# Quantized feed-forward of a decoder: h stored by group, x clipped on GpSimd, neighbouring products interleaved

## The chip, the cores and the metric

One core of one Trainium2 chip runs the whole program in one launch. The metric is the device time of that core in microseconds, the median of several runs. Engines are named as the profile names them: PE (TensorE), DVE (VectorE), ACT (ScalarE), POOL (GpSimd) and SP (SyncE).

## The reference

The model is a chain of six layers on x of 64 x 128 x 128 (batch, tokens, width), each `x = layernorm(x + layer(x))`. The change touches the last layer alone, a feed-forward in which activations and weights are rounded to 8-bit steps. The scale of an activation is one number for the whole tensor, so its maximum must be known before any of it is rounded:

```
def _act_fake_quant(x, clip_factor):
    scale = sigmoid(clip_factor) * max(abs(x)) / 127
    return clip(round(x / scale), -128, 127) * scale
def _weight_fake_quant(w):                      # one scale a row
    scale = max(abs(w), axis=1, keepdims=True) / 127
    return clip(round(w / scale), -128, 127) * scale
xq   = _act_fake_quant(x, clip_x)
gate = xq @ wq(w_gate).T ; up = xq @ wq(w_up).T       # 128 -> 352
h    = _act_fake_quant(silu(gate) * up, clip_down)    # needs the maximum over all h
y    = h @ wq(w_down).T                               # 352 -> 128
x    = layernorm(x + y)
```

## The kernel before, in words

The layers run one after the other; `quantized` is the last. All of its x (64 batches) stays in SBUF with tokens on the partitions: `xs` is [128 tokens, 64, 128]. The work is cut into NG = 16 groups of GB = 4 batches, GT = 512 columns a group. The inner width 352 is cut into IC = 3 chunks of up to 128 rows.

After the weights are rounded and the scale of x is known (`scale_of`, `s_k`), the **first half** runs over the groups. For each group:

- DVE clips x in two passes (`quantize_x`): L2489 multiplies by the inverse scale (a pointer scalar) and takes the minimum with 127 into `xt`; L2491 takes the maximum with -128 and adds a large constant that makes the addition round. There is one `xt`, so group g waits until ACT has read g-1 (`s_xq`).
- ACT subtracts the constant and writes bf16 (`rounded`, L2420, into `xqb`); PE turns it (`turned`, L2360); ACT copies it out of the bank (`copied`, L2414, into `xT`, two buffers).
- PE makes gate and up products of chunk c in banks 2 + 2c and 3 + 2c (`gate_up`, L2367 and L2368). It waits until the up product on DVE of the same chunk of the group before has freed the banks (`s_h`).
- ACT takes tanh of half the gate (L2426, into `th`, one buffer a chunk, also freed by `s_h`).
- DVE multiplies (tanh + 1) by the gate product from its bank into `t1` (L2541, the gate product below), then `t1` by a scale and the up product from its bank into h (L2543, the up product below). `t1` is one buffer: the up product waits for the gate product just ahead of it, and the next gate product for that up product.
- DVE takes the largest magnitude of the group's h (L2545).

On ACT the order in a group is tanh 0 to 2, copy of x of g+1, rounding of x of g+2. On DVE it is both passes over x of g+2, then gate and up product of chunk 0, of chunk 1, of chunk 2, then the maximum. POOL has nothing to do in this half. Each engine runs two groups unrolled, then a hardware loop over pairs of groups, then the last two unrolled; inside the loop the counts waited for and the addresses by group are worked out in registers.

h is kept for all groups: `h` is [128, 3 chunks, 8192 tokens] and `hg` its view by group, so a group's h is three runs of 512 in each partition, 8192 apart.

When the last maximum is there, the scale of h is worked out (`prologue2`), and the **second half** runs over the groups again: DVE clips h in two passes as it did x (`shift`, L2562 and L2564, into `ht`, two buffers, one run of 1536 each), ACT rounds to bf16 (`whole`, L2447), PE makes the down product (`down`, L2391), DVE scales it out of the bank (L2574), POOL adds it to x (`add`, L2609), DVE takes mean and variance (`stats`: L2584, L2589, L2593, L2594), POOL makes the inverse root with a pow (L2614) and the shift with a multiply (L2617), ACT applies them (`normed`, L2454, four groups later), and SP stores the group. DVE's order in a group g is `shift` of g+1, the scaling of g, `stats` of g-1; POOL's is `add` of g, then pow and multiply of g-1.

Of the kernel before, what the change touches and what calls it, by code (L numbers as in the profile page):

```python
# [9 lines left out]
ALU = mybir.AluOpType  # L10
ACT = mybir.ActivationFunctionType
AX = mybir.AxisListType
# [2222 lines left out]
def quantized(nc, const, banks, x, y, a):  # L2235
# [13 lines left out]
    with ExitStack() as st:  # L2249
        def sb(name, shape, dt=F32):  # L2250
            return st.enter_context(nc.sbuf_tensor(f"q_{name}", shape, dt))

        def sem(name, per=1):
            return Count(nc.alloc_semaphore(f"q_{name}"), per)
# [25 lines left out]
        xqb = sb("xqb", [P, GT], BF16)  # L2280
        xT = sb("xT", [P, 2, GT], BF16)
        th = sb("th", [P, IC, GT])
        t1 = sb("t1", [P, GT])
        h = sb("h", [P, IC, B * S])
        ht = sb("ht", [P, 2, IC, GT])
        hq = sb("hq", [P, 2, IC, GT], BF16)
        r = sb("r", [P, 2, GT])
# [5 lines left out]
        s_w = sem("weights"); s_setup = sem("setup"); s_sig = sem("sigmoid_exp"); s_wq = sem("weights_quantized")  # L2293
        s_wt = sem("weights_turned", 2); s_wT = sem("weights_copied", 2); s_top = sem("top", 3); s_tt = sem("top_turned", 3)
        s_t1 = sem("top_reduced", 3); s_tb = sem("top_spread", 3); s_k = sem("scales_ready")
        s_xs = sem("x_shifted"); s_xq = sem("x_quantized"); s_hm = sem("h_max"); s_xt = sem("x_turned"); s_xT = sem("x_copied")
        s_gu = sem("gate_up", IC); s_th = sem("tanh", IC); s_h = sem("h", IC)
        s_hs = sem("h_shifted"); s_hq = sem("h_quantized"); s_y = sem("down"); s_yr = sem("down_read"); s_add = sem("x_added")
        s_bn = sem("out_stats"); s_ag = sem("out_mean"); s_ov = sem("out_var"); s_pw = sem("out_pow"); s_op = sem("out_scales")
# [8 lines left out]
        o_g = y.rearrange("(g b) t d -> g t b d", b=GB)  # L2308
        xg = xs[:].rearrange("p (g b) d -> p g (b d)", b=GB)
        xs_g = xs[:].rearrange("p (g b) d -> p g b d", b=GB)  # L2310
        hg = h[:].rearrange("p c (g t) -> p g c t", t=GT)
        block = st.enter_context(nc.Block())

        @block.sync
# [152 lines left out]
        def _(dve):  # L2467
# [16 lines left out]
                v.reciprocal(inv[:, n:n + 1], scl[:, n:n + 1]).then_inc(ch.sem, 1)  # L2484
                v.wait_ge(ch.sem, ch.next())

            def quantize_x(v, ch, g):
                v.wait_ge(s_xq.sem, s_xq.at(g))
                v.tensor_scalar(xt[:], xg[:, g, :], inv[:, 0:1], QMAX, ALU.mult, ALU.min).then_inc(ch.sem, 1)  # L2489
                v.wait_ge(ch.sem, ch.next())  # L2490
                v.tensor_scalar(xt[:], xt[:], -QMAX - 1.0, MAGIC, ALU.max, ALU.add).then_inc(s_xs.sem, 1)  # L2491

            def prologue(v, ch):
                v.wait_ge(s_w.sem, 16 * NW)
                v.wait_ge(s_setup.sem, s_setup.at(1))
                v.tensor_reduce(wamax[:, 0:2 * IC], wgu[:], AX.X, ALU.max, apply_absolute_value=True)
                v.tensor_reduce(wamax[:, 2 * IC:], wd[:], AX.X, ALU.max, apply_absolute_value=True).then_inc(ch.sem, 1)
                v.wait_ge(ch.sem, ch.next())
                v.tensor_scalar(wscale[:], wamax[:], 1.0 / QMAX, None, ALU.mult).then_inc(ch.sem, 1)
                v.wait_ge(ch.sem, ch.next())  # L2500
                v.reciprocal(winv[:], wscale[:]).then_inc(ch.sem, 1)
                v.wait_ge(ch.sem, ch.next())
                for c in range(2 * IC):
                    whole(v, ch, wq[:, c, :], wgu[:, c, :], wgu[:, c, :], winv[:, c:c + 1]).then_inc(ch.sem, 1)
                    v.wait_ge(ch.sem, ch.next())
                whole(v, ch, wdq[:], wd[:], wd[:], winv[:, 2 * IC:]).then_inc(ch.sem, 1)
                v.wait_ge(ch.sem, ch.next())
                for n in range(2):
                    ins = v.memset(wq[IL:P, n * IC + 2, :], 0.0)
                ins.then_inc(s_wq.sem, 1)  # L2510
                v.wait_ge(s_sig.sem, s_sig.at(1))
                v.tensor_scalar(sig[:], sig[:], 1.0, None, ALU.add).then_inc(ch.sem, 1)
                v.wait_ge(ch.sem, ch.next())
                v.reciprocal(sig[:], sig[:]).then_inc(ch.sem, 1)
                v.wait_ge(ch.sem, ch.next())
                for c in range(LC):
                    v.wait_ge(s_ld[c].sem, s_ld[c].at(16))
                    ins = v.tensor_reduce(xmax[:, c:c + 1], xs[:, c * B // LC:(c + 1) * B // LC, :].rearrange("p b d -> p (b d)"),  # L2518
                                          AX.X, ALU.max, apply_absolute_value=True)
                ins.then_inc(ch.sem, 1)  # L2520
                v.wait_ge(ch.sem, ch.next())
                scale_of(v, ch, 0, xmax[:])
                v.tensor_scalar(kt[:], wscale[:, 0:IC], scl[:, 0:1], 0.5, ALU.mult, ALU.mult).then_inc(ch.sem, 1)
                v.wait_ge(ch.sem, ch.next())
                v.tensor_scalar(kk[:], wscale[:, IC:2 * IC], scl[:, 0:1], None, ALU.mult).then_inc(ch.sem, 1)
                v.wait_ge(ch.sem, ch.next())
                v.tensor_tensor(kk[:], kk[:], kt[:], ALU.mult).then_inc(s_k.sem, 1)
                v.wait_ge(s_k.sem, s_k.at(1))
                quantize_x(v, ch, 0)
                quantize_x(v, ch, 1)  # L2530

            def turn(v, ch, i):
                last = isinstance(i, int) and i == TURNS - 1
                for l in range(2):
                    g = 2 * i + l
                    if not last:
                        quantize_x(v, ch, g + 2)
                    for c in range(IC):
                        v.wait_ge(s_th.sem, s_th.at(g, c + 1))
                        v.wait_ge(s_h.sem, s_h.at(g, c))  # L2540
                        v.scalar_tensor_tensor(t1[:], th[:, c, :], 1.0, banks[2 + 2 * c], ALU.add, ALU.mult).then_inc(ch.sem, 1)  # L2541
                        v.wait_ge(ch.sem, ch.next())
                        v.scalar_tensor_tensor(hg[:, g, c, :], t1[:], kk[:, c:c + 1], banks[3 + 2 * c], ALU.mult, ALU.mult).then_inc(s_h.sem, 1)  # L2543
                    v.wait_ge(s_h.sem, s_h.at(g + 1))
                    v.tensor_reduce(hmax[:, bass.ds(g, 1)] if not isinstance(g, int) else hmax[:, g:g + 1],  # L2545
                                    hg[:, g, :, :], AX.XY, ALU.max, apply_absolute_value=True).then_inc(s_hm.sem, 1)
            looped(dve, s_dve, TURNS, 2 * (1 + IC), prologue, turn, lambda v, ch: None)

            def prologue2(v, ch):
                v.wait_ge(s_hm.sem, s_hm.at(NG))  # L2550
# [47 lines left out]
        def _(pool):  # L2598
# [4 lines left out]
            pool.memset(magic[:], -MAGIC).then_inc(s_pool, 1)  # L2603
            pool.wait_ge(s_pool, 3)
            pool.sem_inc(s_setup.sem, 1)
            def add(g, l):
                pool.wait_ge(s_yr.sem, s_yr.at(g + 1))
                pool.sem_inc(s_step, 1)
                pool.tensor_tensor(xg[:, g, :], xg[:, g, :], r[:, l], ALU.add).then_inc(s_add.sem, 1)  # L2609

            def scales(g, l):
                pool.wait_ge(s_ov.sem, s_ov.at(g + 1))
                pool.sem_inc(s_step, 1)
                pool.tensor_tensor(osc[:, g, 0, :], ovar[:, l, 0, :], half_pow[:, 0:GB], ALU.pow).then_inc(s_pw.sem, 1)  # L2614
                pool.wait_ge(s_pw.sem, s_pw.at(g + 1))
                pool.sem_inc(s_step, 1)
                pool.tensor_tensor(osc[:, g, 1, :], osc[:, g, 0, :], ovar[:, l, 1, :], ALU.mult).then_inc(s_op.sem, 1)  # L2617
            add(0, 0)
            add(1, 1)
            scales(0, 0)  # L2620
# [119 lines left out]
```

## Time and profile before

| what | value |
|---|---|
| median of 3 runs (lowest to highest) | 5442.49 us (5440.62 to 5445.76) |
| profiled execution, its time | 5428.83 us |
| profiled execution, span of the core | 5427.1 us |
| busy over the span: DVE / PE / POOL / ACT | 4319.6 (80%) / 4056.8 (75%) / 3163.7 (58%) / 2781.0 (51%) us |
| first half of the last stage, from the scale of x to the last maximum of h | 5208.9 to 5332.5 us |
| second half, to the end of the span | 5332.5 to 5427.0 us |

The profile is of one execution. Most of the span belongs to the five layers ahead; the two last lines are the stretches that the change touches. A busy share over the whole span says little about them, so they are read by stretch and in order of time.

### The profile page before, as it was taken

How to read it: one execution, taken by the hardware profiler on the slowest of the kernel's cores; microseconds unless marked ns; L12 is line 12 of the kernel's file. 1: busy time of each engine (PE TensorE's matmuls, PEld its weight loads, DVE VectorE, ACT ScalarE, POOL GpSimd, SP SyncE). 2: the span in 40 equal slices, each digit the busy share in tenths (PEclk: the TensorE clock that was granted, in tenths of full speed). 3: DMA queues.
4: the chain of work that ended last, by engine and by line, in shares of the span. 5: the costliest groups of instructions: out<-in, count | busy, mean ns of one | idle time of the engine just before them, and what ended most of it. 6: DMA issues, size and time to landing. Idle time of an engine off the chain costs nothing. (4 is left out here: it accounts for less than half of the span.)

```text
span 5427.1 us, 104523 instructions
## 1 busy us (share of the span) xinstructions
PE 4056.8 (75%) x29692; PEld 2331.6 (43%) x29692; DVE 4319.6 (80%) x8453; ACT 2781.0 (51%) x6469; POOL 3163.7 (58%) x3426
## 2 busy tenths in 40 slices
PE   5878778887787778874888678883747788688843
PEld 2333333333333333332666456652735666466611
DVE  5999999999999999994888767763356777666678
ACT  4555555555555555552777534434654445344434
POOL 5888888878888888874777533326452222333302
PEclk8998999889989989986999889995877888799955
DMA  2111111111110111102655366544125555465511
GB/s 84 67 49 54 69 68 68 42 62 69 68 69 33 69 68 68 69 37 46 105 102 102 60 119 110 104 88 151 57 89 107 95 96 95 82 112 102 98 39 31
DMA packets 320209, 420.99 MB, mean 78 GB/s; under 512 B 40000, under 2 KB 301712, under 8 KB 309136
## 3 DMA queue, kind: packets, MB, share of 16 engines
q1 hardware_dynamic: 315536, 408.35, 32.3%
q0 software_dynamic: 4352, 8.95, 0.5%
q8 instruction: 128, 2.10, 0.2%
q14 instruction: 193, 1.58, 0.1%
HBM read 307.65 MB, written 109.58 MB: 77 GB/s over the span
## 5 line engine op out<-in xcount | busy, mean ns | idle before, releaser
L2202 POOL TENSOR_TENSOR m_h<-m_dtu,m_Bb 128x512 f32<-128x512 f32 x1024 | 1598.1, 1590 | 148.4 <-PE bank L1835 146.1
L1835 PE MATMUL bank<-m_h,ident 128*128 128x512 f32 x2048 | 1245.2, 699 | 404.5 <-DVE m_h L2101 398.8
L1835 PEld LDWEIGHTS bank<-m_h,ident 128*128 128x128 f32 x2048 | 370.6, 210 | 1083.8 <-DVE m_h L2101 931.3
L2095 DVE TENSOR_TENSOR_SCAN m_h<-m_dA,m_h 128x512 f32<-128x512 f32 x512 | 771.0, 1506 | 0.5
L2101 DVE TENSOR_TENSOR m_h<-m_h,bank 128x512 f32<-128x512 f32 x1024 | 672.1, 656 | 14.4 <-PE bank L1828 14.4
L2095 DVE TENSOR_TENSOR_SCAN m_h<-bank,m_h 128x512 f32<-128x512 f32 x512 | 620.4, 1212 | 16.5 <-ACT bank L1983 9.5
L1983 ACT ACTIVATE bank<-m_dt,m_A 128x512 f32<-128x512 f32 x512 | 352.5, 688 | 378.6 <-DVE m_h L2095 273.6
L1983 ACT ACTIVATE m_dA<-m_dt,m_A 128x512 f32<-128x512 f32 x512 | 366.9, 717 | 350.1 <-DVE m_h L2095 343.4
L688 DVE TENSOR_REDUCE x_nm<-bank 128x4 f32<-128x308 f32 x512 | 242.7, 474 | 184.0 <-PE bank L359 181.1
L531 ACT ACTIVATE x_sm<-bank,x_nm 128x77 f32<-128x77 f32 x1024 | 318.2, 336 | 62.5 <-DVE x_nm L688 62.1
L688 DVE TENSOR_REDUCE f_nm<-bank 128x4 f32<-128x512 f32 x256 | 175.7, 687 | 120.2 <-PE bank L359 119.1
L521 ACT ACTIVATE a_pT<-bank 128x512 f32<-128x512 f32 x256 | 152.9, 598 | 219.5 <-PE bank L379 217.0
L1779 PE MATMUL bank<-m_xTp,m_wck 128*128 128x512 f32 x512 | 255.0, 602 | 12.6 <-ACT m_xTp L1897 12.6
L521 ACT ACTIVATE f_pT<-bank 128x512 f32<-128x512 f32 x256 | 153.0, 598 | 216.4 <-PE bank L379 215.7
L521 ACT ACTIVATE x_pT<-bank 77x512 f32<-77x512 f32 x256 | 151.9, 593 | 216.5 <-PE bank L379 213.6
L896 POOL TENSOR_TENSOR x_var<-x_var,half_pow 128x1 f32<-128x1 f32 x128 | 70.5, 550 | 304.2 <-DVE x_var L742 304.2
L876 POOL TENSOR_TENSOR x_sm<-x_sm,x_gp 128x308 f32<-128x308 f32 x256 | 203.1, 798 | 71.9 <-ACT x_sm L531 71.4
L401 PE MATMUL bank<-x_pT,x_vB 128*32 128x128 f32 x4096 | 220.3, 288 | 6.9 <-ACT x_ou L540 6.6
L896 POOL TENSOR_TENSOR a_var<-a_var,half_pow 128x1 f32<-128x1 f32 x64 | 35.3, 551 | 324.8 <-DVE a_var L742 324.8
L688 DVE TENSOR_REDUCE a_nm<-bank 128x4 f32<-128x512 f32 x256 | 175.2, 685 | 60.5 <-PE bank L359 45.8
L531 ACT ACTIVATION_READ_ACCUMULATOR x_sm<-bank,x_nm 128x1 f32 x1024 | 221.6, 216 | 0.0
L1828 PE MATMUL bank<-m_Cs,m_selC 80*128 80x512 bf16 x512 | 213.5, 417 | 0.0
(425 smaller groups left out, 10366.2 us busy)
## 6 DMA issues: line engine op xcount, KB each, us to landing
m_Bb<-m_B SPq DMA_DIRECT2D x32, 4096.0 KB, 12.2
x_Ks<-x_k_parts SPq DMA_DIRECT2D x32, 462.0 KB
x_q_parts<-x_qp SPq DMA_DIRECT2D x32, 384.0 KB, 4.0
x_Qs<-x_q_parts SPq DMA_DIRECT2D x32, 384.0 KB
f_Ks<-f_k_parts SPq DMA_DIRECT2D x16, 768.0 KB
a_Ks<-a_k_parts SPq DMA_DIRECT2D x16, 768.0 KB
x_xp<-x_stage SPq DMA_DIRECT2D x32, 256.0 KB
x_Qs<-x_q_parts SPq DMA_DIRECT2D x32, 256.0 KB
```

Source lines behind the costliest of these rows:

```text
L401: ins = pe.matmul(bankO[j * VT:(j + 1) * VT, half * S:(half + 1) * S], vB[:, lb % 2, 4 * c + j, :], pT[:, lb % 2, 4 * c + j, :], start=(c ...
L521: act.activation(pT[0:sk, p, 4 * c:4 * c + 4, :].rearrange("p h t -> p (h t)"), src, ACT.Exp).then_inc(s_e.sem, 1)
L531: ins = act.activation(sm[:, lm % 2, h, :], bankS[c % 2][:, (h - 4 * c) * S2:(h - 4 * c + 1) * S2], ACT.Exp, bias=nm[:, lm % 2, 0, h:h + 1 ...
L688: v.tensor_reduce(nm[:, p, 0, 4 * c:4 * c + 4], src, AX.X, ALU.max, negate=True).then_inc(ready.sem, 1)
L876: pool.tensor_tensor(ws, ws, gp[:, lm // GB, lm % GB, :].unsqueeze(1).to_broadcast([P, 4, S2]), ALU.mult).then_inc(s_pg.sem, 1)
L1779: ins = pe.matmul(o, wck[:, d, part, c * P:(c + 1) * P], xTp[:, :, part:part + S], start=(part == 0), stop=(part == CK - 1))
L1828: pe.matmul(banks[2 + s % 2], selC[:, s, :], Cs[:, d, :], start=True, stop=True).then_inc(s_C.sem, 1)
L1835: pe.matmul(banks[4 + c], ident[:], h[:, k % RING, :], start=(s == 0), stop=(s == NS - 1)).then_inc(s_ya.sem, 1)
L1983: act.activation(decays[k % AHEAD], dt[:, d, c, :], ACT.Exp, scale=A[:, d, c, s:s + 1]).then_inc(s_dA.sem, 1)
L2095: v.tensor_tensor_scan(h[:, k % RING, :], decays[k % AHEAD], h[:, k % RING, :], 0.0, ALU.mult, ALU.add).then_inc(s_h.sem, 1)
L2101: v.tensor_tensor(h[:, k % RING, :], h[:, k % RING, :], banks[2 + s % 2], ALU.mult).then_inc(s_hC.sem, 1)
L2202: pool.tensor_tensor(h[:, k % RING, :], dtu[:, d, c, :], Bb[:, d, s, :], ALU.mult).then_inc(s_dB.sem, 1)
```

## The change: what it does

- `h` is allocated as [128, group, chunk, 512] in place of [128, chunk, 8192]: a group's h is one run of 1536 in each partition. The view `hg` is that tensor now.
- `quantize_x` moves from DVE to POOL, with the same two passes and one more semaphore (`s_xc`) between them. POOL waits for the scales (`s_k`) and then runs all 16 groups, unrolled, before its part of the second half. `xt` remains one buffer.
- `t1` gets one buffer a chunk. DVE's order in a group becomes gate 0, maximum of the group before, gate 1, up 0, gate 2, up 1, up 2. The last maximum follows after the loop.
- The gate product of chunk c now waits for `s_h` of the same chunk of the group before.

```diff
-        t1 = sb("t1", [P, GT])
-        h = sb("h", [P, IC, B * S])
+        t1 = sb("t1", [P, IC, GT])
+        hg = sb("h", [P, NG, IC, GT])
...
-        hg = h[:].rearrange("p c (g t) -> p g c t", t=GT)
...
-            def quantize_x(v, ch, g):            # and its calls on DVE
-                v.wait_ge(s_xq.sem, s_xq.at(g))
-                v.tensor_scalar(xt[:], xg[:, g, :], inv[:, 0:1], QMAX, ALU.mult, ALU.min).then_inc(ch.sem, 1)
-                v.wait_ge(ch.sem, ch.next())
-                v.tensor_scalar(xt[:], xt[:], -QMAX - 1.0, MAGIC, ALU.max, ALU.add).then_inc(s_xs.sem, 1)
...
+            def largest(v, g):
+                v.wait_ge(s_h.sem, s_h.at(g + 1))
+                v.tensor_reduce(hmax[:, bass.ds(g, 1)] if not isinstance(g, int) else hmax[:, g:g + 1],
+                                hg[:, g, :, :], AX.XY, ALU.max, apply_absolute_value=True).then_inc(s_hm.sem, 1)
 
             def turn(v, ch, i):
-                last = isinstance(i, int) and i == TURNS - 1
                 for l in range(2):
                     g = 2 * i + l
-                    if not last:
-                        quantize_x(v, ch, g + 2)
-                    for c in range(IC):
+                    ready = [None] * IC
+
+                    def times_gate(c):
                         v.wait_ge(s_th.sem, s_th.at(g, c + 1))
-                        v.wait_ge(s_h.sem, s_h.at(g, c))
-                        v.scalar_tensor_tensor(t1[:], th[:, c, :], 1.0, banks[2 + 2 * c], ALU.add, ALU.mult).then_inc(ch.sem, 1)
-                        v.wait_ge(ch.sem, ch.next())
-                        v.scalar_tensor_tensor(hg[:, g, c, :], t1[:], kk[:, c:c + 1], banks[3 + 2 * c], ALU.mult, ALU.mult).then_inc(s_h.sem, 1)
-                    v.wait_ge(s_h.sem, s_h.at(g + 1))
-                    v.tensor_reduce(...)
-            looped(dve, s_dve, TURNS, 2 * (1 + IC), prologue, turn, lambda v, ch: None)
+                        v.wait_ge(s_h.sem, s_h.at(g - 1, c + 1))
+                        v.scalar_tensor_tensor(t1[:, c, :], th[:, c, :], 1.0, banks[2 + 2 * c], ALU.add, ALU.mult).then_inc(ch.sem, 1)
+                        ready[c] = ch.next()
+
+                    def times_up(c):
+                        v.wait_ge(ch.sem, ready[c])
+                        v.scalar_tensor_tensor(hg[:, g, c, :], t1[:, c, :], kk[:, c:c + 1], banks[3 + 2 * c], ALU.mult, ALU.mult).then_inc(s_h.sem, 1)
+
+                    times_gate(0)
+                    if not (isinstance(g, int) and g == 0):
+                        largest(v, g - 1)
+                    for c in range(1, IC):
+                        times_gate(c)
+                        times_up(c - 1)
+                    times_up(IC - 1)
+            looped(dve, s_dve, TURNS, 2 * IC, prologue, turn, lambda v, ch: largest(v, NG - 1))
...
+            def quantize_x(g):                   # on POOL
+                pool.wait_ge(s_xq.sem, s_xq.at(g))
+                pool.tensor_scalar(xt[:], xg[:, g, :], inv[:, 0:1], QMAX, ALU.mult, ALU.min).then_inc(s_xc.sem, 1)
+                pool.wait_ge(s_xc.sem, s_xc.at(g + 1))
+                pool.tensor_scalar(xt[:], xt[:], -QMAX - 1.0, MAGIC, ALU.max, ALU.add).then_inc(s_xs.sem, 1)
...
+            pool.wait_ge(s_k.sem, s_k.at(1))
+            pool.sem_inc(s_step, 1)
+            for g in range(NG):
+                quantize_x(g)
             add(0, 0)
             add(1, 1)
```

## Rows read from the trace of the kernel before

**Rows 1.** The two halves: us, each engine's busy us (instructions), clock, DMA share, GB/s

```profile
5208.90:5332.50 123.60, 56.09 (x160) 14.73 (x160) 108.99 (x146) 52.23 (x80) 0.00 (x0) 0.50 0.00 0
...
5332.50:5427.00 94.50, 25.12 (x198) 20.35 (x198) 78.11 (x215) 50.06 (x80) 39.83 (x48) 0.50 0.16 45
```

**Rows 2.** DVE's groups in both halves: count, busy us, mean ns, idle before, releaser

```profile
L2543 DVE SCALAR_TENSOR_TENSOR q_h<-q_t,q_kk,bank 128x512 f32 (+1 forms) x48 | 35.9, 747 | 6.2 <-DVE q_t L2541 5.7
L2541 DVE SCALAR_TENSOR_TENSOR q_t<-q_th,bank 128x512 f32<-128x512 f32 x48 | 32.9, 686 | 4.2 <-ACT q_th L2426 0.7
L2562 DVE TENSOR_SCALAR q_ht<-q_h,q_inv 128x1536 f32 (+1 forms) x16 | 29.0, 1810 | 1.2 <-issue 1.1
L2545 DVE TENSOR_REDUCE q_hmax<-q_h (+1 forms) x16 | 28.1, 1753 | 1.8
L2564 DVE TENSOR_SCALAR q_ht<-q_ht 128x1536 f32<-128x1536 f32 x16 | 15.4, 960 | 0.6
```

**Rows 3.** DVE's timeline, one steady group of the first half: start us, us

```profile
5241.09 1.75 DVE L2545 TENSOR_REDUCE q_hmax<-q_h  x1
...
5243.28 0.43 DVE L2491 TENSOR_SCALAR q_xt<-q_xt 128x512 f32<-128x512 f32 x1
5243.62 0.68 DVE L2541 SCALAR_TENSOR_TENSOR q_t<-q_th,bank 128x512 f32<-128x512 f32 x1
5244.46 0.75 DVE L2543 SCALAR_TENSOR_TENSOR q_h<-q_t,q_kk,bank 128x512 f32 x1 [0.16 <-DVE q_t L2541]
...
5248.75 1.75 DVE L2545 TENSOR_REDUCE q_hmax<-q_h  x1
```

**Rows 4.** Timeline of PE and ACT after an up product of chunk 0

```profile
5245.26 0.61 PE L2367 MATMUL bank<-q_xT,q_wT 128*128 128x512 bf16 x1 [2.78 <-DVE q_h L2543]
5245.66 0.63 PE L2368 MATMUL bank<-q_xT,q_wT 128*128 128x512 bf16 x1
5246.33 0.69 ACT L2426 ACTIVATE q_th<-bank,q_kt 128x512 f32<-128x512 f32 x1 [1.87 <-PE bank L2368]
```

**Rows 5.** Timeline of the first half's start, from the first pass over x

```profile
5208.95 0.49 DVE L2489 TENSOR_SCALAR q_xt<-q_x,q_inv 128x512 f32<-128x512 f32 x1
...
5211.96 0.71 ACT L2420 ACTIVATE q_xqb<-q_xt,q_magic 128x512 bf16<-128x512 f32 x1
...
5213.19 0.69 ACT L2426 ACTIVATE q_th<-bank,q_kt 128x512 f32<-128x512 f32 x1 [0.52 <-PE bank L2368]
...
5213.91 0.69 DVE L2541 SCALAR_TENSOR_TENSOR q_t<-q_th,bank 128x512 f32<-128x512 f32 x1 [0.26 <-ACT q_th L2426]
```

**Rows 6.** POOL's groups over the whole span: an addition, a pow, a memset

```profile
L2609 POOL TENSOR_TENSOR q_x<-q_x,q_r 128x512 f32 x14 | 17.8, 1270 | 26.1 <-DVE q_r L2574 26.1
...
L2614 POOL TENSOR_TENSOR q_osc<-q_ovar,half_pow 128x4 f32 x14 | 14.3, 1020 | 5.4 <-DVE q_ovar L2594 5.4
...
L1442 POOL MEMSET moe_go_on<- 128x512 f32 x1 | 0.5, 525 | 0.1
```

**Rows 7.** Timeline of one steady group of the second half

```profile
5353.44 1.81 DVE L2562 TENSOR_SCALAR q_ht<-q_h,q_inv 128x1536 f32 x1
5353.77 1.02 POOL L2614 TENSOR_TENSOR q_osc<-q_ovar,half_pow 128x4 f32 x1 [0.41 <-DVE q_ovar L2594]
...
5355.29 0.96 DVE L2564 TENSOR_SCALAR q_ht<-q_ht 128x1536 f32<-128x1536 f32 x1
...
5358.71 1.81 DVE L2562 TENSOR_SCALAR q_ht<-q_h,q_inv 128x1536 f32 x1 [0.22 <-issue]
```

**Rows 8.** Timelines of two earlier stages where DVE and POOL run together

```profile
3119.16 1.15 POOL L848 TENSOR_TENSOR f_qp<-f_qr,f_qp 128x512 bf16<-128x512 f32 x1
3119.23 1.36 DVE L654 CAST f_qp<-f_qr 128x512 bf16<-128x512 f32 x1 [1.04 <-POOL f_qr L841]
...
3674.49 1.01 POOL L1450 TENSOR_TENSOR moe_scales<-moe_norm,half_pow 128x4 f32 x1
3674.70 0.17 DVE L1272 TENSOR_SCALAR moe_norm<-moe_stats 128x4 f32<-128x4 f32 x1 [0.26 <-DVE moe_stats L1266]
```

More of the change, by code:

```diff
@@ L2295, in quantized @@
         s_t1 = sem("top_reduced", 3); s_tb = sem("top_spread", 3); s_k = sem("scales_ready")
-        s_xs = sem("x_shifted"); s_xq = sem("x_quantized"); s_hm = sem("h_max"); s_xt = sem("x_turned"); s_xT = sem("x_copied")
+        s_xc = sem("x_clipped"); s_xs = sem("x_shifted"); s_xq = sem("x_quantized"); s_hm = sem("h_max"); s_xt = sem("x_turned"); s_xT = sem("x_copied")
         s_gu = sem("gate_up", IC); s_th = sem("tanh", IC); s_h = sem("h", IC)
@@ L2527, in prologue @@
                 v.tensor_tensor(kk[:], kk[:], kt[:], ALU.mult).then_inc(s_k.sem, 1)
-                v.wait_ge(s_k.sem, s_k.at(1))
-                quantize_x(v, ch, 0)
-                quantize_x(v, ch, 1)
+            def largest(v, g):
+                v.wait_ge(s_h.sem, s_h.at(g + 1))
+                v.tensor_reduce(hmax[:, bass.ds(g, 1)] if not isinstance(g, int) else hmax[:, g:g + 1],
+                                hg[:, g, :, :], AX.XY, ALU.max, apply_absolute_value=True).then_inc(s_hm.sem, 1)
@@ L2532, in turn @@
             def turn(v, ch, i):
-                last = isinstance(i, int) and i == TURNS - 1
                 for l in range(2):
                     g = 2 * i + l
-                    if not last:
-                        quantize_x(v, ch, g + 2)
-                    for c in range(IC):
+                    ready = [None] * IC
+                    def times_gate(c):
                         v.wait_ge(s_th.sem, s_th.at(g, c + 1))
-                        v.wait_ge(s_h.sem, s_h.at(g, c))
-                        v.scalar_tensor_tensor(t1[:], th[:, c, :], 1.0, banks[2 + 2 * c], ALU.add, ALU.mult).then_inc(ch.sem, 1)
-                        v.wait_ge(ch.sem, ch.next())
-                        v.scalar_tensor_tensor(hg[:, g, c, :], t1[:], kk[:, c:c + 1], banks[3 + 2 * c], ALU.mult, ALU.mult).then_inc(s_h.sem, 1)
-                    v.wait_ge(s_h.sem, s_h.at(g + 1))
-                    v.tensor_reduce(hmax[:, bass.ds(g, 1)] if not isinstance(g, int) else hmax[:, g:g + 1],
-                                    hg[:, g, :, :], AX.XY, ALU.max, apply_absolute_value=True).then_inc(s_hm.sem, 1)
```

## The prediction, made before the result was known

> **What bounds the kernel now.** The change touches only the last stage, the quantized feed-forward. Its work after the scale of x falls into two halves, the last 218 us of the span [rows 1]. In the first (123.6 us: gate and up products, all maxima) DVE works 109.0 us, ACT 52.2, PE 56.1 and POOL nothing. In the second (94.5 us: rounding h, the down product, the norm) DVE works 78.1, ACT 50.1, POOL 39.8. The reader should see in both that DVE is the engine with no time to spare and that POOL is free in the first. TensorE's granted clock is 0.50 in both, its 1.2 GHz level. The groups by line [rows 2] say what DVE does there: in the first half, for each of 16 groups, three gate products of 0.686 us, three up products of 0.747, one maximum of 1.753, and two passes over x; in the second, the clip of h at 1.810 and its second pass at 0.960, though both treat 1536 elements a partition.
>
> DVE's order of time for one steady group [rows 3] shows a period of 7.66 us, 5241.09 to 5248.75. Two things make it: 0.48 + 0.43 us for x ([rows 5] has the first pass, [rows 3] the second), and gaps. Where nothing has to be waited for, the next instruction starts about 0.08 before the last one's end (5243.28 + 0.43 = 5243.71, next start 5243.62). Where the up product waits for the gate product just ahead, it starts 0.16 after the end instead (5243.62 + 0.68 to 5244.46). The group has three such pairs.
>
> **The change part by part: first half.**
>
> *x to POOL.* 32 passes leave DVE: 0.43 + 0.345 (0.43 less the 0.08 of overlap, as for the next) + 0.085 of hand-over between them, 0.86 us a group.
>
> *Interleaving and the late maximum.* The up product now follows the next chunk's gate product, and the maximum of group g-1 stands behind the first gate product of g, so no DVE instruction waits for the one just ahead. The group becomes a sum of unwaited starts: 3 x 0.686 + 3 x 0.747 + 1.753 - 7 x 0.08 = 5.49 us. t1 grows to one buffer a chunk, so its reuse no longer waits either.
>
> *What is late next.* Bank pair 0 and th 0 come free when up product 0 ends. From there [rows 4]: PE starts 0.06 later (5245.26 after an end at 5244.46 + 0.75 [rows 3]), its second product ends 1.03 after that, ACT's tanh starts 0.04 later and takes 0.69, and about 0.05 hands it to DVE: 1.87 us. Meanwhile DVE has gate 2, up 1 and up 2 left, 0.606 + 0.667 + 0.667 = 1.94. That is nearly a tie: the ring of up 0, PE, tanh, gate 0, maximum, gate 1, up 0 is also 5.5 us round. Chunks 1 and 2 have over 3 us. The copy and the rounding of x stand ahead of that tanh on ACT: tanh 2 ends 1.85 us after the group's start by [rows 4], the copy is no longer than a tanh, the rounding takes 0.71 [rows 5], so ACT is free at about 3.25, before up 0 ends at 3.63. A tie with register waits in a loop will not be met each time; I take 5.6, with 5.49 below and 5.95 above (the 0.16 stall back at each of three gate products).
>
> *POOL's passes.* No pass with one tensor input at 128x512 f32 by POOL stands in the trace. The nearest rows [rows 6]: a memset of that shape 0.525 us, an addition of two tensors 1.27. I take 0.9, the middle. The Trainium skill, GPSIMD Engine Reference, section Engine selection, holds that POOL is about half as fast as DVE on two inputs but near line rate on one; an estimate from that would be about 0.5 us a pass and 1 us less at the start; no row here shows it. In the loop POOL needs 2 x 0.9, ACT's rounding 0.72 (xt has one buffer) and some 0.2 of hand-over, 2.7 of 5.6 us: hidden. DVE's instructions in this half each read at most one tensor from SBUF besides the bank, and none shows the halved time of a clip pass, so I let them and POOL run beside each other at their own durations. Not hidden is the start. POOL begins where DVE did (5208.95), but ACT has the rounding of group 1 ahead of the first tanh, and it now waits for four POOL passes and two roundings: 5208.95 + 4 x 0.9 + 2 x 0.72 + 0.5 of hand-overs = 5214.5, against 5213.19 [rows 5]. That is 1.3 us late (0.15 at 0.525 a pass, 2.8 at 1.27).
>
> *Sum of the half.* First gate product at 5213.91 + 1.3 = 5215.2; group 1 starts 4.1 later (gate 1 waits for a tanh 0.85 behind the first, the pace of a PE pair; then 0.606 + 0.747 to the end of up 0 and 1.87 for the ring); 14 periods of 5.6 are 78.4; the last group and its maximum, which now has nothing behind it, 5.6 + 1.75 = 7.35: end at 5305.1. Before, the half ended at 5332.5 [rows 1]. Saved: 27.4 us (bounds: 5.49 and 0.15, 30.1; 5.95 and 2.8, 21.0).
>
> **The change: second half.** With h as [group, chunk, token], the clip reads one run of 1536 where it read three runs of 512, 8192 apart, while its destination is one run as before. The second pass, one run in and out, takes 0.960, just over half the clip's 1.810 [rows 2]; and x, one run too, was clipped with the same pointer scalar in 0.48 where the pass with constants took 0.43 [rows 5, 3]. So the clip should take 0.960 + 0.05 = 1.01: 0.80 less. A group lasts 5.27 (5353.44 to 5358.71 [rows 7]; of 16, every other one is some 0.2 shorter), nearly all DVE; without 0.80 it is some 4.35. ACT's work there is 50.1/16 = 3.1 a group and POOL's 39.8/16 = 2.5, so DVE stays the limit. Of 16 clips that of group 1 is lost in a wait for the first down product; 15 x 0.80 = 12.0.
>
> What speaks against it is POOL. The pow of the norm starts 0.33 us after the clip does [rows 7]. At the old rate they ran side by side. At the halved rate DVE and POOL exclude each other in this trace: a CAST of 512 elements, work of some 0.43 (as the second pass over x [rows 3]), took 1.36 behind a POOL tensor_tensor that had started 0.07 before it [rows 8]. But another DVE tensor_scalar, 0.2 us into a pow of the same 128x4 shape, took 0.17 [rows 8]; a pow on four elements mostly computes, so it should give way. I allow 0.07 a group for pow's reads: 11 us saved.
>
> The Trainium skill, SBUF — State Buffer, section Who interferes with whom, is stricter: a DVE instruction in a two-port mode and a POOL instruction exclude each other for the whole instruction, and whoever issues first goes first. By that rule the clip would run, then pow with the second pass waiting for all of it. The CAST row agrees with that, the tensor_scalar inside the pow does not; what it would make of the time is the first rival below.
>
> **Sum.** 27.4 + 11 = 38.4 us. The profiled execution took 5428.83 (span 5427.1 and 1.7 around it), so it would take 5390. The median of the runs, 5442.49, lies 13.7 above that execution; nothing in the rows ties that difference to this stage, so I carry it: 5404.
>
> **Rivals.**
>
> 1. *POOL's pow holds the second half.* Pow waits for the clip (1.01), then the second pass waits for pow's 1.02: the group gains 0.80 and loses about 1.02, 0.2 x 15 = 3 us worse than before in that half. For: the CAST row. Against: the tensor_scalar row. Saved 27.4 - 3 = 24: 5418.
> 2. *The ring takes DVE's place in the first half.* Each hand-over in the loop costs 0.1 to 0.2 more (ACT and PE wait on registers too), period 6.2: 14 x 0.6 = 8.4 less saved, 30.0: 5412. For: the tie above, and the 0.16 gaps. Against: [rows 4] already hold the loop's hand-overs.
> 3. *The slower side: POOL's clip is too slow.* The group is then 2T + 0.72 + 0.2. It passes the old 7.66 at T = 3.4 us a pass, and at 3.7 it eats the second half's gain too. For: pow takes 1.02 us for four elements [rows 6], so POOL can be slow by operation. Against: multiply-, add- or subtract-like tensor_tensors keep 1.27 for 512. At T = 5: 16 x 3.3 = 52 lost, 11 gained: 5483.
> 4. *The clip doesn't change its rate* (the layout was not the reason): 27.4 saved, 5415.
>
> **How the numbers follow.** Forecast 0.62 (own range 5398 to 5410), rival 1 0.16, rival 2 0.11, rival 3 0.03, rival 4 0.05, rivals 1 and 2 together 0.03 (27.4 - 8.4 - 3 = 16 saved, 5426). Both halves at their best, 30.1 + 12.0, give 5400; the three runs spread over 5 us, so the range begins at 5397, and it ends with rivals 1 and 2 together, 5425. A measurement can tell about 0.2%, 11 us, from no change. All cases but rival 3 save more than that; faster 0.95, same 0.02, slower 0.03.
>
> **What would show it.** DVE's idle before the up products (5.7 us before) near zero and none of its passes on x; starts of successive maxima 5.5 to 5.7 apart; first tanh 1 to 2 us later after the scales; POOL's passes 0.5 to 1.3 each; the clip of h at about 1.01 and groups of the second half 4.3 to 4.5 apart, with pow lengthened instead. A second pass of h of about 2 us shows rival 1; DVE idle before the first gate product of each group, released by tanh, shows rival 2; ACT's rounding waiting for POOL throughout, rival 3; a clip of 1.8 with no POOL beside it, rival 4. The prediction is wrong if the first half saves under 21 us or the second loses.

## The result, and the profile after

The changed kernel took 5410.6 us, the median of six runs (5403.87 to 5429.04), against 5444.12 for the kernel before on the same chip (six runs, 5434.42 to 5452.83). The ratio is 0.9943 with a 95% interval of 0.9925 to 0.9961: 0.6% less time, a small gain but clear of no change. The forecast was 5404, its range 5397 to 5425.

Runs of either kernel scatter by some 20 us, most of it from the layers ahead: in ten of the eleven traces the scales of the last stage come anywhere from 5204.8 to 5232.8 us, while the changed kernel's two traces agree within 0.1 us in each half. So the two halves of the last stage are compared inside each trace. One run, the version without interleaving below, took 6430.81 us with its layers ahead at a lower granted clock (0.55 over the whole run, 0.87 in the others), and only its last stage is read. The first fence answers to [rows 1]: each stretch, busy us of PE, PEld, DVE, ACT and POOL with instructions, granted clock, DMA share, GB/s.

```profile
5218.46:5318.40 99.94, 51.36 (x160) 16.05 (x160) 87.75 (x113) 50.52 (x80) 62.89 (x32) 0.57 0.00 0
5318.40:5402.13 83.73, 25.13 (x198) 20.36 (x198) 66.57 (x215) 50.03 (x80) 49.14 (x48) 0.50 0.18 50
```

The first half went from 123.55 to 99.91 us, the second from 94.66 to 83.76 (ends taken to the nanosecond): 23.6 and 10.9, together 34.5. POOL, idle in the first half before, now works 62.9 us of it. The groups of the changed kernel answer to [rows 2] and, for POOL, to [rows 6].

```profile
L2540 DVE SCALAR_TENSOR_TENSOR q_h<-q_t,q_kk,bank 128x512 f32 (+1 forms) x48 | 34.2, 741 | 0.0
L2535 DVE SCALAR_TENSOR_TENSOR q_t<-q_th,bank 128x512 f32<-128x512 f32 x48 | 32.6, 680 | 12.1 <-ACT q_th L2425 11.5
L2610 POOL TENSOR_SCALAR q_xt<-q_x,q_inv 128x512 f32<-128x512 f32 x16 | 32.0, 2002 | 45.1 <-DVE q_kk L2520 26.1 <-ACT q_xqb L2419 18.9
L2612 POOL TENSOR_SCALAR q_xt<-q_xt 128x512 f32<-128x512 f32 x16 | 30.9, 1929 | 1.4
L2564 DVE TENSOR_SCALAR q_ht<-q_h,q_inv 128x1536 f32 (+1 forms) x16 | 16.4, 1027 | 1.3 <-issue 1.1
L2566 DVE TENSOR_SCALAR q_ht<-q_ht 128x1536 f32<-128x1536 f32 x16 | 16.3, 1019 | 0.5
```

The idle time before the up products (L2540) is gone, 6.2 us before; the clip of h (L2564) takes 1.03 for 1.81. But a pass over x takes POOL 2.00 and 1.93 us, and DVE idles 12.1 before gate products. Most of that is one wait, at the start. The timeline there answers to [rows 5]: start us, us, idle before in brackets.

```profile
5218.69 2.00 POOL L2610 TENSOR_SCALAR q_xt<-q_x,q_inv 128x512 f32<-128x512 f32 x1 [26.12 <-DVE q_kk L2520]
...
5225.71 1.93 POOL L2612 TENSOR_SCALAR q_xt<-q_xt 128x512 f32<-128x512 f32 x1
...
5227.67 0.72 ACT L2419 ACTIVATE q_xqb<-q_xt,q_magic 128x512 bf16<-128x512 f32 x1 [2.78 <-POOL q_xt L2612]
5228.30 1.82 ACT L2425 ACTIVATE q_th<-bank,q_kt 128x512 f32<-128x512 f32 x3
...
5229.00 1.28 DVE L2535 SCALAR_TENSOR_TENSOR q_t<-q_th,bank 128x512 f32<-128x512 f32 x2 [10.54 <-ACT q_th L2425]
...
5232.54 0.72 ACT L2419 ACTIVATE q_xqb<-q_xt,q_magic 128x512 bf16<-128x512 f32 x1 [1.93 <-POOL q_xt L2612]
```

The first tanh waits for four POOL passes and two roundings. The first gate product comes 10.54 us after the scales; before it was 5.0. Group 1 is late as well: on ACT the rounding of group 2's x stands ahead of group 1's tanh, and it waits 1.93 us for POOL's third pair of passes.

Two groups further on stand for the steady state; they answer to [rows 3 and 4].

```profile
5259.52 0.61 PE L2366 MATMUL bank<-q_xT,q_wT 128*128 128x512 bf16 x1 [1.88 <-DVE q_h L2540]
...
5259.98 1.40 DVE L2540 SCALAR_TENSOR_TENSOR q_h<-q_t,q_kk,bank 128x512 f32 x2
5260.69 0.69 ACT L2425 ACTIVATE q_th<-bank,q_kt 128x512 f32<-128x512 f32 x1 [1.65 <-PE bank L2367]
...
5261.52 0.69 DVE L2535 SCALAR_TENSOR_TENSOR q_t<-q_th,bank 128x512 f32<-128x512 f32 x1
...
5265.18 0.39 PE L2366 MATMUL bank<-q_xT,q_wT 128*128 128x512 bf16 x1 [2.09 <-DVE q_h L2540]
...
5265.64 1.40 DVE L2540 SCALAR_TENSOR_TENSOR q_h<-q_t,q_kk,bank 128x512 f32 x2
5265.82 0.69 ACT L2425 ACTIVATE q_th<-bank,q_kt 128x512 f32<-128x512 f32 x1 [1.26 <-PE bank L2367]
...
5266.95 0.68 DVE L2535 SCALAR_TENSOR_TENSOR q_t<-q_th,bank 128x512 f32<-128x512 f32 x1
```

Follow chunk 0 twice. At the 1.2 GHz level a product takes 0.61; the tanh that needs the pair ends at 5260.69 + 0.69 = 5261.38, when DVE's last up product is just over (5259.98 + 1.40), and gate 0 starts 0.14 later. In the next group the product takes 0.39, the tanh ends at 5266.51, and gate 0 starts 0.09 before its predecessor's end. But the clock is only one of two things that decide. Here are the stretches from maximum to maximum, these two groups and the one ahead of them:

```profile
5251.02:5256.47 5.45, 3.37 (x11) 1.04 (x10) 5.45 (x9) 3.23 (x6) 3.85 (x3) 0.50 0.00 0
5256.47:5262.12 5.65, 3.55 (x12) 1.13 (x11) 5.51 (x8) 3.27 (x6) 4.23 (x3) 0.50 0.00 0
5262.12:5267.55 5.43, 2.69 (x12) 0.84 (x11) 5.43 (x8) 3.36 (x6) 3.83 (x3) 0.81 0.00 0
```

The first stretch is at 0.50 too, and yet it is 5.45 long. There the tanh of chunk 0 follows PE's second product more closely:

```profile
5254.47 0.63 PE L2367 MATMUL bank<-q_xT,q_wT 128*128 128x512 bf16 x1
...
5255.14 0.69 ACT L2425 ACTIVATE q_th<-bank,q_kt 128x512 f32<-128x512 f32 x1 [1.46 <-PE bank L2367]
```

It starts 0.04 after that product's end and ends at 5255.83, 0.10 before DVE's last up product, so gate 0 has nothing to wait for. In the group of 5.65 it starts 0.13 after the product. This goes by the place in the hardware loop, each turn of which does two groups: all through the loop's twelve groups the tanh of a turn's first group starts 0.13 after PE, that of its second 0.04. So the tie that the prediction named is there. It is lost in the first group of a turn at 0.50 (5.65 or 5.66 us, four of the six). It is won where PE made chunk 0's products at the 2.4 GHz level (the other two), and in the second group of every turn at either clock (5.43 to 5.45). Before, the whole half was at 0.50 [rows 1].

The second half shows one odd group and two steady ones; they answer to [rows 7].

```profile
5328.52 1.01 DVE L2564 TENSOR_SCALAR q_ht<-q_h,q_inv 128x1536 f32<-128x1536 f32 x1
5328.78 1.86 POOL L2617 TENSOR_TENSOR q_x<-q_x,q_r 128x512 f32<-128x512 f32 x1 [26.86 <-DVE q_r L2576]
5329.56 1.90 DVE L2566 TENSOR_SCALAR q_ht<-q_ht 128x1536 f32<-128x1536 f32 x1
...
5337.99 1.02 DVE L2564 TENSOR_SCALAR q_ht<-q_h,q_inv 128x1536 f32 x1
5338.31 1.73 POOL L2622 TENSOR_TENSOR q_osc<-q_ovar,half_pow 128x4 f32 x1 [0.41 <-DVE q_ovar L2596]
5339.05 0.96 DVE L2566 TENSOR_SCALAR q_ht<-q_ht 128x1536 f32<-128x1536 f32 x1
...
5342.46 1.05 DVE L2564 TENSOR_SCALAR q_ht<-q_h,q_inv 128x1536 f32 x1 [0.23 <-issue]
5342.50 1.05 POOL L2622 TENSOR_TENSOR q_osc<-q_ovar,half_pow 128x4 f32 x1 [0.36 <-DVE q_ovar L2596]
5343.55 0.96 DVE L2566 TENSOR_SCALAR q_ht<-q_ht 128x1536 f32<-128x1536 f32 x1
5343.81 0.75 POOL L2625 TENSOR_TENSOR q_osc<-q_osc,q_ovar 128x4 f32 x1 [0.26 <-POOL q_osc L2622]
```

Steady groups come in two kinds, in turn. In the first, POOL's pow starts 0.32 into the clip and takes 1.73. It ends 1.03 us after the clip does, as long as a whole pow of before (1.02), but also 0.03 after the second pass, which ran at its own 0.96 beside it; these rows don't tell for which of the two it waited. In the second kind pow starts 0.04 after the clip does, and both take 1.05, so neither waited more than 0.03 for the other. There the multiply behind pow is the one that is longer, 0.75 for 0.20, and it ends 0.05 after the second pass. In both kinds POOL waits, and DVE's passes keep their time within 0.03. Groups last 4.28 and 4.47 in turn, 5.04 and 5.26 before. The odd group is the third: there POOL's first addition, 512 elements, starts inside the clip, and the second pass takes 1.90. That happens once and costs 0.9 us.

### The profile page after: what moved, and what is told of

Its sections match the earlier page's. It is cut to its first block and busy times, and to the rows that moved or that the text cites. A ratio compares the mean times of both kernels' runs of the same rounds, so it can differ in the third digit from the quotient of the medians.

```text
span 5402.1 us, 104475 instructions
## 1 busy us (share of the span) xinstructions
PE 4058.6 (75%) x29692; PEld 2332.1 (43%) x29692; DVE 4293.4 (79%) x8421; ACT 2777.7 (51%) x6469; POOL 3230.1 (60%) x3458
## 6 DMA issues: line engine op xcount, KB each, us to landing
m_Bb<-m_B SPq DMA_DIRECT2D x32, 4096.0 KB, 12.1
```

## The experiments

Each is a version of the changed kernel. Where only one execution was taken, its total says little (the scatter above), so the verdicts go by the stretches in its trace, from the scales to the last maximum and from there to the end, in us. Steady groups are those of the hardware loop; "5.43 or 5.66" stands for 5.43 to 5.46 and 5.64 to 5.67.

| run | first half | second half | steady group, first half |
|---|---|---|---|
| before | 123.55 | 94.66 | 7.66 |
| changed | 99.91 | 83.76 | 5.43 or 5.66 |
| first three groups of x on DVE | 93.42 | 83.72 | 5.43 or 5.66 |
| all of x on DVE | 103.47 | 83.70 | 6.29 |
| gate and up of a chunk together | 105.24 | 83.77 | 5.91 |
| old layout of h | 99.82 | 94.59 | 5.43 or 5.66 |
| maximum in its own group | 100.68 | 83.71 | 5.65 |
| other operations in POOL's passes | 99.05 | 83.77 | 5.43 or 5.66 |
| an addition ahead of pow | 99.90 | 103.08 | 5.43 or 5.66 |
| first three on DVE, up 0 earlier | 92.18 | 83.72 | 5.43 |
| changed, again | 99.85 | 83.77 | 5.43 or 5.66 |

**The start.** DVE does both passes for groups 0 to 2 ahead of its loop, POOL the rest.

```diff
+    FIRST = 3
...
+                for g in range(FIRST):
+                    quantize_v(v, ch, g)         # DVE, after kk
...
-            for g in range(NG):
+            for g in range(FIRST, NG):
                 quantize_x(g)                    # POOL
```

> The changed kernel with x of groups 0, 1 and 2 clipped by DVE at the start as in the kernel before, POOL from group 3 on. Theory: POOL's passes of 2.0 us cost only at the start (first gate product 10.5 us after the scales where it was 5.0), and are hidden from group 2 on: the first half goes from 99.9 us to about 94 (first gate product at 5.0, group 1 no longer waiting for POOL), second half unchanged at 83.8. Rival: POOL's passes hold the loop too (2 x 2.0 + 0.72 + hand-overs is 4.9 of 5.5 us): the first half gains at the start and loses it again, 97 or more.

```profile
5227.94 0.69 DVE L2545 SCALAR_TENSOR_TENSOR q_t<-q_th,bank 128x512 f32<-128x512 f32 x1 [0.26 <-ACT q_th L2426]
```

The first gate product is back at 5.00 us after the scales (they end at 5222.94), from there group 1's comes 4.12 later in place of 4.87, and the steady groups are what they were. The half is 93.42, 6.5 us less: the start cost the changed kernel 5.5 us ahead of the first gate product and 0.75 in the group after. The other 0.2 is the tie, won once more in this trace (group 2 at 5.43 in place of 5.66). POOL's two passes cost nothing once the loop runs.

**All of x on DVE.** The new order and layout, with both passes at the head of each group on DVE, POOL none.

```diff
+                    if not last:
+                        quantize_v(v, ch, g + 2)
...
                     times_gate(0)
...
-            for g in range(NG):
-                quantize_x(g)                    # POOL
```

> The changed kernel with all passes over x on DVE again (at the head of the group, as before); order of products, late maximum and layout as changed. Theory: DVE is the limit of the first half, so its 0.86 us a group comes back: period about 6.3 where it was 5.5, first gate product again 5.0 us after the scales, first half about 104 us (changed kernel 99.9, before 123.5). So the move of x alone is worth about 4 us, most of what it saves in the loop being given back at the start. Rival: the ring of bank pair 0 through PE and tanh is the limit, the 0.86 us lies in its shadow: period 5.6, first half about 93.

```profile
5214.17:5317.64 103.47, 51.12 (x158) 16.30 (x160) 100.56 (x144) 50.72 (x80) 0.00 (x0) 0.57 0.00 0
```

The order, with t1's three buffers, alone saves 20.1 of the first half's 23.6 us: groups of 6.29. The passes cost DVE 0.86 a group, 6.29 - 5.43, as the prediction had it. POOL's part in the changed kernel is the other 3.6: some 10 saved in the loop (103.47 to 93.42 without the late start), 6.5 lost at the start.

**No interleaving.** Gate and up product of a chunk stand together again; the late maximum and the three buffers of t1 stay.

```diff
-                    for c in range(1, IC):
-                        times_gate(c)
-                        times_up(c - 1)
-                    times_up(IC - 1)
+                    times_up(0)
+                    for c in range(1, IC):
+                        times_gate(c)
+                        times_up(c)
```

> The changed kernel with gate and up product of a chunk again one after the other (the maximum of the group before still between the first pair, t1 one buffer a chunk). Theory: two pairs a group start their up product 0.16 after the gate product's end in place of 0.08 before it, 0.24 each: period about 5.45 + 0.48 = 5.9, first half about 106 us. Rival: the stall at the pairs was only what hid ACT and PE, and the period is the ring's: it stays at 5.5 and the first half at 100.

DVE's timeline, with the idle time before the up products in brackets:

```profile
6270.01 0.68 DVE L2535 SCALAR_TENSOR_TENSOR q_t<-q_th,bank 128x512 f32<-128x512 f32 x1
6270.84 0.75 DVE L2540 SCALAR_TENSOR_TENSOR q_h<-q_t,q_kk,bank 128x512 f32 x1 [0.15 <-DVE q_t L2535]
```

The group is 5.91, 0.48 more than 5.43: two pairs (chunk 0 has the maximum in between) of 0.24, the 0.15 of idle time and the 0.08 by which instructions that wait for nothing overlap. The new order shortens a group by 1.37 in all (7.66 less 0.86 for x is 6.80, down to 5.43). This run gives 0.48 of that to the two pairs; the other 0.89 belongs to chunk 0's pair, the late maximum and the three buffers of t1 together, which no run here separates fully.

**The old layout of h.** Only the allocation and the view are those of before.

```diff
-        hg = sb("h", [P, NG, IC, GT])
+        h = sb("h", [P, IC, B * S])
+        hg = h[:].rearrange("p c (g t) -> p g c t", t=GT)
```

> The changed kernel with h laid out by chunk again (three runs of 512, 8192 apart), all else as changed. Theory: the layout alone halves the clip of h: clip back at 1.81, second half back at 94.6 us (changed 83.8), first half unchanged at 99.9 within 0.3. Rival: the clip is quicker because of what POOL and DVE do beside each other, not of the layout: second half stays near 84.

```profile
5330.42 1.81 DVE L2565 TENSOR_SCALAR q_ht<-q_h,q_inv 128x1536 f32 x1
5330.74 1.02 POOL L2623 TENSOR_TENSOR q_osc<-q_ovar,half_pow 128x4 f32 x1 [0.42 <-DVE q_ovar L2597]
...
5332.27 0.96 DVE L2567 TENSOR_SCALAR q_ht<-q_ht 128x1536 f32<-128x1536 f32 x1
```

The clip is back at 1.81, pow runs beside it at its own 1.02, and the second half is that of before within 0.1 us. The layout is all of the second half's gain and touches nothing in the first.

**The maximum at the end of its own group.**

```diff
                     times_gate(0)
-                    if not (isinstance(g, int) and g == 0):
-                        largest(v, g - 1)
...
                     times_up(IC - 1)
+                    largest(v, g)
```

> The changed kernel with each group's maximum at the end of its own group again; products interleaved as changed. Theory: the maximum now waits for the up product just ahead of it (about 0.2 a group), while bank pair 0 gets the maximum's 1.75 us of room more, so no group waits for tanh whatever TensorE's clock: all groups about 5.65 apart, first half about 101.5 us (changed: 5.43 or 5.66, 99.9). Rival: the ring through PE and tanh was not what made the groups of 5.66: they stay 0.2 apart from each other and the first half is about 103.

```profile
5265.67 1.40 DVE L2540 SCALAR_TENSOR_TENSOR q_h<-q_t,q_kk,bank 128x512 f32 x2
5267.20 1.75 DVE L2524 TENSOR_REDUCE q_hmax<-q_h  x1
```

Every group in the loop is 5.65, at either clock: the maximum now starts 0.13 after the up product it needs (5265.67 + 1.40 = 5267.07), 0.2 in all, and gate 0, with the maximum ahead of it, never waits. So the late maximum bought 0.77 us in the whole half: in the first group of each turn, where the clock is at 1.2 GHz, it only exchanges one wait for the other.

**What POOL takes by operation.** Two groups each of x go through other operations of the same shape (or of half the width), so x isn't the reference's in those; groups 0, 1, 14 and 15 stay as they were. The branches of the code are summed up in comments here.

```diff
+                kind = g // 2
-                pool.tensor_scalar(xt[:], xg[:, g, :], inv[:, 0:1], QMAX, ALU.mult, ALU.min)
+                # kind 1: mult by inv alone, then an addition alone
+                # kind 2: tensor_tensor of x with itself; 3: min alone, then max alone
+                # kind 4: mult and add with constants; 5: half the width; 6: copy
```

> POOL's passes over x in other forms by pairs of groups: groups 2 and 3 with one operation a pass, 4 and 5 with a product of two tensors as first pass, 6 and 7 with one operation with a constant, 8 and 9 with multiply and add of constants, 10 and 11 half as wide, 12 and 13 a copy as first pass; x is then not what the reference has. Theory: the 2.0 us go by operations and elements: about 1.1 us with one operation, 1.27 for the product, about 1.05 for half the width, a copy under 0.8. Rival: a tensor_scalar on POOL costs 2.0 whatever it does: 1.9 to 2.0 with one operation, and half the width near 1.05 all the same.

POOL's groups by line: shortest, median and longest ns, start of the first and the last.

```profile
L2623 POOL TENSOR_SCALAR q_xt<-q_x,q_inv x6: 1149/2002/2007, 5233.1 to 5311.3; 128x512 f32<-128x512 f32 x4, 128x256 f32<-128x256 f32 x2
L2613 POOL TENSOR_SCALAR q_xt<-q_x,q_inv x2: 1568/1571/1574, 5242.9 to 5246.9; 128x512 f32<-128x512 f32 x2
L2627 POOL TENSOR_SCALAR q_xt<-q_xt x2: 1492/1492/1493, 5244.5 to 5248.5; 128x512 f32<-128x512 f32 x2
L2615 POOL TENSOR_TENSOR q_xt<-q_x x2: 1039/1039/1039, 5250.9 to 5256.2; 128x512 f32<-128x512 f32 x2
L2617 POOL TENSOR_SCALAR q_xt<-q_x x2: 1488/1490/1493, 5261.5 to 5267.1; 128x512 f32<-128x512 f32 x2
L2619 POOL TENSOR_SCALAR q_xt<-q_x x2: 617/618/618, 5272.5 to 5278.1; 128x512 f32<-128x512 f32 x2
L2621 POOL COPY q_xt<-q_x x2: 609/610/610, 5294.8 to 5300.3; 128x512 f32<-128x512 f32 x2
```

In this order: multiply and minimum 2.00 (1.15 at half width, so 0.85 for 256 elements more); a multiply alone 1.57; an addition alone 1.49; a product of a tensor with itself 1.04; a minimum alone 1.49; multiply (by 1.0) and add with two constants 0.62; a copy 0.61. Neither side had this: one operation is not 1.1, two are not 2.0 whatever they do, and two with constants took less than half of one alone. The first passes, when DVE is idle, take 2.0 as those in the loop do. So it is POOL's own time for the operation, not a resource shared with DVE. The run also bears out what made group 1 late in the changed kernel: group 2's passes took 1.57 + 1.49 here in place of 2.00 + 1.93, 0.87 less, and group 1 came 4.00 after group 0 in place of 4.87.

**An addition of 128x512 on POOL ahead of each pow.** It works on a tile of its own.

```diff
+                pool.tensor_tensor(wide[:, 1, :], wide[:, 0, :], wide[:, 0, :], ALU.add).then_inc(s_wide.sem, 1)
+                pool.wait_ge(s_wide.sem, s_wide.at(g + 2))
...
                 pool.tensor_tensor(osc[:, g, 0, :], ovar[:, l, 0, :], half_pow[:, 0:GB], ALU.pow)
```

> The changed kernel with an addition of two tensors of 128x512 on POOL ahead of each pow of the second half (on tiles of its own; nothing reads it). Theory: at the halved rate DVE's clip shuts POOL out, and a POOL instruction that streams shuts DVE out for its whole length, while a pow on four elements does not: the addition waits for the clip, then the second pass over h waits for the addition, 0.96 to about 2.2 us; groups 4.4 to about 5.6, second half 83.8 to about 102. Rival: DVE goes first whenever it is ready, and the second pass stays at 0.96: second half at most 86.

```profile
5325.48 1.01 DVE L2565 TENSOR_SCALAR q_ht<-q_h,q_inv 128x1536 f32 x1
5325.74 1.64 POOL L2626 TENSOR_TENSOR q_wide<-q_wide 128x512 f32<-128x512 f32 x1 [0.28 <-DVE q_ovar L2597]
5326.52 1.68 DVE L2567 TENSOR_SCALAR q_ht<-q_ht 128x1536 f32<-128x1536 f32 x1
...
5335.41 1.26 POOL L2621 TENSOR_TENSOR q_x<-q_x,q_r 128x512 f32 x1 [0.41 <-issue]
5335.69 1.01 DVE L2596 TENSOR_SCALAR q_ovar<-q_ost 128x4 f32<-128x4 f32 x1
```

Now every second pass from the fourth group on takes 1.68, and groups last 5.42 and 5.74, 1.2 more than in the changed kernel: the second half loses 19.3 us and is slower than before's. The second pass makes 0.72 of the 1.2. Most of the rest is a consequence that the expectation didn't have: POOL's addition to x now comes later, beside the statistics, and a DVE instruction on four elements there, 0.19 us in the changed kernel, takes 0.77 in the median and in the group shown 1.01, ending 0.03 after the addition. This is the prediction's first rival, made real by an operation that streams 512 elements in place of one on four.

**The improvement that the runs point to.** The first experiment, and chunk 0's up product right behind the maximum, so that its banks are asked for again earlier. It was run six times, and the changed kernel six times beside it.

```diff
                     times_gate(0)
                     largest(v, g - 1)            # not for g = 0
-                    for c in range(1, IC):
-                        times_gate(c)
-                        times_up(c - 1)
-                    times_up(IC - 1)
+                    times_up(0)
+                    times_gate(1)
+                    times_gate(2)
+                    times_up(1)
+                    times_up(2)
```

> The kernel of the run with the first three groups' x quantized on VectorE, and with one more change: the order on TensorE in a group is gate 0, the maxima of the group before, up 0, gate 1, gate 2, up 1, up 2. Theory (the groups of 5.66 us come from the pair of chunk 0's banks, which is asked for again before its product h is read out, whenever TensorE is at its 1.2 GHz level): chunk 0's up product now ends earlier, its h is read earlier, and every group takes about 5.43 us at either clock; the first half 92.2 us (93.42 without the new order), the second half 83.7, together about 176, which is 42 below the kernel before (218.2) and 7.7 below the changed kernel (183.7): a median about 7 to 8 us under the changed kernel's in the same runs, near 5402. Rival (the longer groups come from the tanh or from VectorE's own hand-overs): groups of 5.66 us stay where the granted clock is 0.5, the first half is 93.4 or more.

> The changed kernel once more, in the same rounds as the version with another order, for the totals side by side. Both theories: first half 99.9, second half 83.8, together 183.7 us within 1; about 34 us under the kernel before, so a ratio near 0.9937.

```profile
5220.70:5312.88 92.18, 50.98 (x158) 16.21 (x160) 89.84 (x119) 50.84 (x80) 51.16 (x26) 0.54 0.00 0
...
5255.00:5275.00 20.00, 12.76 (x39) 4.00 (x38) 20.00 (x26) 11.43 (x18) 15.33 (x8) 0.50 0.00 0
```

From group 1's first gate product on, all 14 distances between groups are 5.43 us, in both groups of a turn and also where the clock is 0.50: in the second stretch DVE is busy 20.00 of 20.00. (Group 1 comes 3.90 after group 0.) The theory of the ring holds, though its condition was too wide: in the changed kernel the clock's lower level alone didn't make a group of 5.66. DVE has nothing left to wait for in the loop. The median is 5400.47 us (5387.32 to 5410.02, six runs) against 5445.4 for before (eleven runs): ratio 0.9918, interval 0.9899 to 0.9937. The changed kernel again had 5414.89, ratio 0.9945 (0.9928 to 0.9961). The two intervals overlap; by the traces the version is 183.6 - 175.9 = 7.7 us better.

## Why the prediction came out as it did

**Second half: the mechanism right, the size in part by luck.** 11 us forecast, 10.90 measured. The clip at 1.03 (1.01 forecast), groups of 4.37 on average (4.35), pow or the multiply behind it lengthened instead of the second pass. The experiment with the old layout shows the cause. The forecast was 12.0 less 1 us that it allowed for pow, 0.07 in each group. Pow cost the clip only 0.03 in every other group; the loss of about that size came at one place that the forecast didn't have, POOL's addition in the third group (0.94 us). The row that the prediction set against rival 1, a tensor_scalar on four elements inside a pow [rows 8], was a fair test: an instruction of that shape is held up by an addition (1.01 above), not by a pow. Rival 4 is out, and rival 1 holds for streaming operations alone: in the odd group and with the added addition, not for pow.

The Trainium skill, SBUF — State Buffer, section Who interferes with whom, says that a DVE instruction in a two-port mode and a POOL one exclude each other for the whole instruction, in order of issue. The rows agree for the second pass waiting for an addition (1.68, 1.90) and for pow being held up where it starts 0.32 into the clip (1.73 in place of 1.02). They disagree for the clip and pow that start within 0.04 of each other (1.05 both), and for the second pass beside pow (0.96).

**First half, the loop: right.** 89.9 us forecast from the first gate product to the last maximum, 89.37 measured. Groups of 5.51 on average against 5.6, the last two included; the bound below was 5.49, and 5.43 was reached, since each instruction is some 6 ns shorter (the maximum 1.746 for 1.753) and the overlap a little larger. The tie in the ring of chunk 0 was the right place to look: it decides some 0.2 us a group, and as the forecast said it is not met each time, but in the first group of each turn at 0.50. The forecast took the clock to stay at 0.50; of the six first groups two had chunk 0's products at 2.4 GHz, some 0.4 us in the kernel's favour. Rival 2's 6.2 isn't there. POOL's work is hidden and doesn't lengthen DVE's (0.680 and 0.741 beside it, 0.679 and 0.742 in the run with all of x on DVE and POOL idle).

**First half, the start: wrong in size.** The mis-sized term is POOL's pass, "I take 0.9, the middle", between 0.525 and 1.27. It measured 2.00 and 1.93. Four passes are 7.9 us in place of 3.6, so the first gate product came 5.54 us later than before, not 1.3, and group 1 came 4.87 after it, not 4.1, as ACT had to round group 2's x ahead of group 1's tanh and waited for POOL. That is 4.2 + 0.8 us lost against the forecast; the loop gave back 1.2. So the half saved 23.6 for 27.4, inside the bounds as a whole (21.0 to 30.1), though the term itself was outside its own. Two of the signs that the prediction named failed with it: passes of 0.5 to 1.3, and a first tanh 1 to 2 us later. The error was to take a memset and an addition as the two ends for an operation of another kind. Rows 6 did hold a warning, and rival 3 used it: a pow on four elements takes 1.02, so POOL's time goes by operation.

The Trainium skill, GPSIMD Engine Reference, section Engine selection, puts POOL near line rate on one input, which the prediction estimated at about 0.5 us a pass. That isn't borne out here: it fits the copy and the multiply and add with constants (0.61 and 0.62), not the clip (2.00, 1.93) or a single minimum or addition (1.49).

**The total.** 38.4 us forecast, 34.5 in the stage, 33.5 between the medians (5444.12 - 5410.6). The forecast of 5404 started from 5442.49 and missed by 6.6, 3.9 of it from the stage; the rest is no more than the medians move (before had 5442.49, 5444.12 and 5445.4 in three sets, the second of which includes the first). The upper end of the range, 5425, is 1 us short of the case that it is meant to end with (5426); nothing turns on it.

**What stays open.** When TensorE's clock rises: it stood at 0.50 through this half before (PE busy 56.1 of 123.6 us) and in the version without interleaving (55.4 of 105.2), and had stretches near 1.0 in the changed kernel (51.4 of 99.9, mean 0.57). The busy share over the half doesn't tell them apart, and no run here was made for it. Nor was one made for the 0.09 us by which the tanh of a turn's first group starts later than that of the second, or for why POOL's operations differ as they do; the 0.62 was measured with a multiplier of 1.0 alone.

## What to carry to other kernels

Work moved to a free engine is hidden in the loop but not ahead of it: work out the fill with the new engine's durations, and leave the first groups on the fast engine. A price for an operation that the trace doesn't show has no bound in rows of other operations; widen the range there, or ask what the sum would be at twice the upper row. On an engine without time to spare, let each instruction's input come from two instructions back (0.23 us each here), and find the ring of buffers with the least slack: one changed place in the order freed it.

## What the runs showed of the hardware

POOL's time at 128x512 float32 goes by the operation, not by the number of operations in the instruction: multiply (by 1.0) and add with constants took 0.62 us, an addition alone 1.49, a minimum alone 1.49, multiply by a pointer scalar and minimum 2.00. A DVE clip of h with three runs of 512 a partition took 1.81 and one of 1536 took 1.02, with the same instruction. Whether DVE and POOL exclude each other depends on what POOL does: pow on four elements left DVE's second pass at 0.96, an addition on 512 made it 1.68 to 1.90 and held up even a DVE instruction on four elements, 1.01 in place of 0.19. A wait can go by the place in a hardware loop: in a turn's first group ACT's tanh started 0.13 after the product it needs, in its second 0.04.
